# Layer 3's feed-forward part inside its edge sweep, and the first gathers of each sweep issued in the phase before

## The chip, the cores and the metric

One core of one Trainium2 chip. The time is the device time of one execution in microseconds, the median of three. The program is written engine by engine: TensorE (PE), VectorE (DVE), ScalarE (ACT), GpSimd (POOL) and SyncE (SP), each with its own instructions in a fixed order and semaphores between them.

## What is computed

A graph network on 6250 nodes of 128 features and 106250 directed edges, sorted by destination, self-loops included. Each layer takes h = relu(layernorm(x)) and adds its result to x.

```python
x = x + L0(h, edge_attr_64)            # relu(h[src] + e @ We + be) summed by dst, MLP, batch norm
x = x + L1(h)                          # mean of neighbours, one linear layer
# third layer (L2 in the names): GATv2, 8 heads
m      = leaky_relu(xl[src] + xr[dst] + edge_attr_128 @ W_e, 0.2)
logits = einsum('eho,ho->eh', m, att)
exl    = exp(logits - segment_max(logits, dst)[dst])
out    = segment_sum(xl[src] * exl / (segment_sum(exl, dst)[dst] + 1e-16), dst) + b_att
h2     = layer_norm(h + out, g1, be1)
result = layer_norm(h2 + gelu(h2 @ W1 + b1) @ W2 + b2, g2, be2)
# fourth layer: two GAT convolutions (4 heads, then 1) with elu behind each
```

## The kernel before

The edges are cut into 208 groups of 512 (four tiles of 128). Five sweeps walk over them, and between or inside them the work by nodes is done: `term_sweep` (first layer), `norm1_phase`, `sum_sweep` (second), `soft_sweep` for number 2 (the third layer, GATv2), `ffn_phase` (its feed-forward part), and `soft_sweep` for numbers 3 and 4 (`narrow_layers`, from L529). "Layer 3's sweep" is below the sweep of number 2.

Every sweep is a software pipeline in steps. At step t each engine does its part for group t, and later parts for groups t-1 to t-8 (LAG = 7). `sweep16` (L138) writes the first steps out, then a loop of 16 steps a round, then the rest. The order inside a step is the order of the code in the function `step` of that engine, written by hand. Four groups make a batch (BATCH), for which logits, running maxima and exponentials are taken together, one lane a head and group, 32 lanes for 8 heads.

POOL only gathers: for each tile an indirect DMA brings 128 source rows (L1792), into a ring of 16 groups. It waits until the group 16 back has been used (`message`).

In layer 3's sweep, TensorE's step (L1937 to L1977) is:

- `edge_terms(t)`: four transposes of gathered rows (L1867), then the matmul of edge attributes (L1873, 128x512) and that of destination rows (L1874).
- `scatter(t-7)`: four matmuls of one-hot by message into 64 partitions of a bank (L1908).
- `head_logits(t-1)`: one matmul, 32 columns by 512 (L1881).
- `flip_window(t-7)`: after ScalarE has copied the window (L1834), two transposes (L1930, L1931). VectorE adds the result to `sums` (`add`, L2016).
- once a batch: a shift (L1940), a carry (L1956), the weights turned edge-major (L1963) and factors (L1969, L1970).

VectorE's step is: leaky ReLU of t-1 (L2075), `add(t-8)`, `weigh(t-7)` (L2066), running maxima of the batch, the z-add of t (L2094), and the carry. ScalarE's: copies of weights, z (L1829), window (L1834) and lanes, and the exponentials.

In the sweeps of numbers 3 and 4 work by nodes is already part of the sweep: chunks of 256 nodes, 25 in all (`CN`, `NCH`), one stage of a chunk at a step (`node_steps`, L158). Chunk c may start at step 8(c + 4), since by then no later edge reaches its nodes (`BEHIND` = 4). Such a sweep ends 31 steps after the last group. Layer 3's does not: it ends after LAG more steps, and `ffn_phase` (L2421) works on 13 chunks of 512 nodes.

Each phase ends with `phase_end` (L68): its semaphores are cleared and all engines meet at a barrier. SP waits before it until the tables for the next sweep are stored. Only then does the next phase's first gather start.

## Time and profile before

| | |
|---|---|
| median of 3 runs | 7460.23 us (7456.46 to 7462.33) |
| span of the profiled execution, first to last instruction | 5796.6 us |
| difference, outside the span | 1663.6 us |
| mean granted TensorE clock | 0.779 |
| busy in the span: PE, DVE, ACT, POOL | 79%, 47%, 21%, 69% |
| gathers of layer 3's sweep, first to last | 2282.0 to 3349.9 us |
| then without a gather until | 3621.1 us |

No other time is given for the profiled execution itself; its span is part of an execution like the three timed ones, and sums below are made against that span. The chain of work that ended last is followed only through the last sweeps, so it says nothing about layer 3; the stretches and timelines do.

### The profile page before, as it was taken

To read this page: it belongs to the slowest core of one execution; us is meant where nothing else is said; L and a number is where in the kernel's file an instruction comes from. 1 tells how busy PE (TensorE), PEld (TensorE's weight loads), DVE (VectorE), ACT (ScalarE), POOL (GpSimd) and SP (SyncE) were. 2 spreads that over 40 slices of the span, in tenths; PEclk is the share of its full clock that TensorE was granted. 3 is DMA by queue.
4 is the path that set the end of the run, shared out by engine and by line. 5 is a ranking of instruction groups with operands and counts; after the bars stand their busy time and mean duration, and the time that the engine had idled before them with its cause. 6 is when DMAs were issued, how large, how long until landed. Compare 5 with 4: busy or idle time off the path is not lost. (4 is left out here: it accounts for less than half of the span.)

```text
span 5796.6 us, 89863 instructions
## 1 busy us (share of the span) xinstructions
PE 4596.1 (79%) x21959; PEld 3153.3 (54%) x21959; DVE 2702.8 (47%) x8105; ACT 1216.6 (21%) x3182; POOL 3988.9 (69%) x4207
## 2 busy tenths in 40 slices
PE   5888888657777776999999977687777758887887
PEld 4777777535556564444444433455555535555555
DVE  4222222321111113677777766555555545555555
ACT  2111111221211211222222258111111111111111
POOL 6777777457777775777777700777777747777775
PEclk9999999975555555999999989666666666666665
DMA  5333333244444443555555510455555534444443
GB/s 151 106 105 105 105 104 104 74 150 106 112 114 107 118 114 90 160 165 165 165 165 164 166 38 24 109 114 114 113 114 115 113 77 107 111 109 110 109 111 78
DMA packets 559823, 663.58 MB, mean 114 GB/s; under 512 B 196431, under 2 KB 390909, under 8 KB 558717
## 3 DMA queue, kind: packets, MB, share of 16 engines
q1 hardware_dynamic: 424909, 382.99, 22.2%
q0 software_dynamic: 134640, 277.80, 21.1%
q14 instruction: 207, 1.70, 0.1%
q8 instruction: 67, 1.10, 0.1%
HBM read 580.95 MB, written 86.19 MB: 115 GB/s over the span
## 5 line engine op out<-in xcount | busy, mean ns | idle before, releaser
L1792 POOL DMA_INDIRECT soft_rows<-table,sources x2496 | 2388.6, 957 | 1128.2 <-issue 737.7
L1422 POOL DMA_INDIRECT sum_rows<-table,sources x832 | 785.7, 944 | 343.9 <-issue 249.6
L1088 POOL DMA_INDIRECT term_rows<-table,sources x832 | 791.4, 951 | 289.4 <-issue 289.4
L1923 PE MATMUL psum<-soft_onehot,soft_message 128*128 128x64 f32 x3328 | 647.6, 358 | 107.1 <-DVE soft_message L2066 105.0
L1923 PEld LDWEIGHTS psum<-soft_onehot,soft_message 128*128 128x128 f32 x3328 | 586.1, 266 | 188.0 <-issue 181.8
L1119 PE MATMUL psum<-term_onehot,term_term 128*128 128x64 f32 x1664 | 403.9, 425 | 188.5 <-DVE sums L1171 176.6
L1464 PE MATMUL psum<-sum_onehot,sum_rows 128*128 128x64 f32 x1664 | 360.4, 391 | 222.7 <-DMA sum_rows<-table,sources 218.4
L1119 PEld LDWEIGHTS psum<-term_onehot,term_term 128*128 128x128 f32 x1664 | 370.7, 328 | 242.1 <-issue 242.0
L1165 DVE TENSOR_TENSOR term_term<-psum,term_rows 128x512 f32<-128x512 f32 x208 | 143.9, 692 | 753.0 <-issue 349.0
L1464 PEld LDWEIGHTS psum<-sum_onehot,sum_rows 128*128 128x128 f32 x1664 | 343.5, 304 | 278.0 <-issue 273.8
L1919 PEld LDWEIGHTS psum<-soft_onehot,soft_weights 128*4 128x4 f32 (+1 forms) x3328 | 284.9, 109 | 305.9 <-issue 293.0
L1109 PE MATMUL psum<-L_We,term_attrs 64*128 64x128 f32 x1664 | 430.5, 438 | 8.4 <-DMA term_attrs<-in_ea64T 8.4
L2066 DVE TENSOR_TENSOR soft_message<-soft_rows,psum 128x512 f32<-128x512 f32 x624 | 418.0, 670 | 2.9 <-issue 2.9
L1892 PE MATMUL psum<-soft_onehotT,soft_dst_cols 128*16 128x512 f32 (+1 forms) x416 | 375.4, 1004 | 49.4 <-DMA soft_dst_cols<-adst 49.4
L1109 PEld LDWEIGHTS psum<-L_We,term_attrs 64*128 64x128 f32 x1664 | 370.0, 325 | 56.4 <-issue 28.6
L1919 PE MATMUL psum<-soft_onehot,soft_weights 128*4 128x64 f32 (+1 forms) x3328 | 358.5, 272 | 12.4 <-DVE weight_sums L2011 0.9
L1097 ACT ACTIVATE term_term<-term_term 128x512 f32<-128x512 f32 x208 | 130.9, 630 | 913.0 <-DVE term_term L1165 913.0
L2016 DVE TENSOR_TENSOR sums<-sums,psum 128x64 f32 x624 | 136.7, 219 | 380.3 <-PE psum L1923 320.5
L1898 PE MATMUL psum<-ident,soft_src_cols 128*16 128x128 f32 (+1 forms) x832 | 173.5, 379 | 175.9 <-ACT soft_src_cols L1806 174.5
L1441 ACT ACTIVATE sum_flat<-psum 64x512 f32<-64x512 f32 x208 | 122.7, 590 | 830.9 <-PE psum L1454 826.4
L1503 DVE TENSOR_TENSOR sums<-sums,psum 128x64 f32 x208 | 46.2, 222 | 530.0 <-PE psum L1465 526.8
L1908 PEld LDWEIGHTS psum<-soft_message,soft_onehot 128*64 128x64 f32 x1664 | 188.1, 139 | 139.6 <-issue 138.8
(277 smaller groups left out, 6619.9 us busy)
## 6 DMA issues: line engine op xcount, KB each, us to landing
soft_onehotT<-onehotsT SPq DMA_DIRECT2D x312, 256.0 KB
soft_onehot<-onehots SPq DMA_DIRECT2D x624, 128.0 KB, 2.1
soft_attrs<-in_ea128T SPq DMA_DIRECT2D x208, 256.0 KB
soft_rows<-table,sources POOLq DMA_INDIRECT x2496
term_attrs<-in_ea64T SPq DMA_DIRECT2D x208, 128.0 KB, 2.8
onehots<-term_onehot SPq DMA_DIRECT2D x208, 128.0 KB
sum_onehot<-onehots SPq DMA_DIRECT2D x208, 128.0 KB, 2.7
onehotsT<-sum_flat SPq DMA_DIRECT2D x208, 128.0 KB
```

Source lines behind the costliest of these rows:

```text
L1088: pool.indirect_dma_start(rows[:, k, t, :], None, io.table0[0:NCH * CN], bass.IndirectOffsetOnAxis(sb.sources[:, g * TPG + t:g * TPG + t + ...
L1109: last = pe.matmul(term_bank[g.slot(4)][:, piece(b)], attrs[:, g.slot(AHEAD), piece(b)], sb.L0_We, start=True, stop=True)
L1119: last = pe.matmul(window[q], term[:, g.slot(4), b, :], onehot[:, g.slot(8), b], start=b == 0, stop=b == TPG - 1)
L1422: pool.indirect_dma_start(rows[:, k, t, :], None, io.table1[0:NCH * CN], bass.IndirectOffsetOnAxis(sb.sources[:, g * TPG + t:g * TPG + t + ...
L1464: pe.matmul(window[q], rows[:, g.slot(AROUND), b, 0:D], onehot[:, k, b], start=b == 0, stop=b == TPG - 1)
L1792: pool.indirect_dma_start(rows[:, k, t, :], None, table[0:NCH * CN], bass.IndirectOffsetOnAxis(sb.sources[:, g * TPG + t:g * TPG + t + 1], ...
L1892: pe.matmul(lane_bank[g.half()], dst_cols[:, j // 2], onehotT[:, pair(g)], start=j == 1, stop=False).then_inc(s.edge_term, 2)
L1898: last = pe.matmul(lane_bank[g.half()][:, piece(b)], src_cols[:, b], sb.ident, start=False, stop=b == TPG - 1)
L1908: last = pe.matmul(window_bank, onehot[:, k, b], message[:, g.slot(2), b, :], start=b == 0, stop=b == TPG - 1)
L1919: pe.matmul(bank[0:H, P:P + W], weights[:, q, b, j::BATCH], onehot[:, k, b], start=b == 0, stop=b == TPG - 1)
L1923: last = pe.matmul(bank[:, 0:W], message[:, g.slot(4), b, :], onehot[:, k, b], start=b == 0, stop=b == TPG - 1)
L2066: v.tensor_tensor(message[:, g.slot(2 if full else 4), :, 0:D].rearrange("p t (h c) -> p t h c", h=H), rows[:, g.slot(AROUND), :, 0:D].rea ...
```

## The change

`soft_sweep` for number 2 becomes a function of its own, `gatv2_sweep`, with `FfnNodes` in place of `ffn_phase`. In it:

- the feed-forward part of a chunk of 256 nodes is 22 stages at steps 8(c + 4) + 2 to + 24; the sweep ends 41 steps after the last group. One PSUM bank (4) is free for it, so
- the logits of a batch are four matmuls taken together, the one of group j writing partitions 32j to 32j + 31 of one bank, and lanes, starts, continuations and maxima use 128 partitions (8 of each 32);
- the scatter's four matmuls go in turn to partitions 0 to 63 and 64 to 127 of the window bank, and the flip is a matmul with `fold` (two identities stacked), which adds the halves;
- weights are turned by matmuls with `quad_pick`, not by transposes; starts and continuations are loaded by four DMAs each instead of one;
- several tiles share space with weights of layers that are done; the one-hot ring has two pairs instead of four.

In all sweeps the ring of gathered rows is one tile for all phases (`Ahead`). Group 0 of the sweeps of numbers 1 to 4 is gathered by POOL at the end of the phase before, once the table is stored, and each such sweep starts with group 1. The wait for the second table (`beside`) stays on SP. The very last tile gathers 16 rows, not 128.

```diff
+class Ahead:
+    def gather(self, pool, g):
+        k = g % AROUND
+        for t in range(TPG):
+            real = slice(0, P if (g * TPG + t) * P < E else 16)
+            pool.indirect_dma_start(self.rows[real, k, t, :], None, self.table,
...
-    soft_sweep(nc, io, sb, 2)
-    ffn_phase(nc, io, sb)
-    soft_sweep(nc, io, sb, 3)
-    soft_sweep(nc, io, sb, 4)
...
+        gatv2_sweep(nc, io, sb, to2, to3)
+        to4 = Ahead(nc, sb, ring, "soft4", io.table4, D + 1)
+        soft_sweep(nc, io, sb, 3, to3, to4)
+        soft_sweep(nc, io, sb, 4, to4, None)
...
             @block.gpsimd
             def _(pool):
-                for g in range(G):
+                for g in range(1, G):
...
+                nodes.table_stored(pool)
+                ahead.gather(pool, 0)
...
+class FfnNodes:
+    def act_steps(self, act, t):
+        node_steps(act, t, (2, self.stage), (4, self.norm1.take_root), (6, self.normalise1), (7, self.scaled1), (8, self.gelus(0)), (9, self.gelus(1)),
+                   (12, self.copy_res), (13, self.norm2.take_root), (14, self.normalise2), (19, self.norm3.take_root), (20, self.normalise3),
+                   (21, self.copy_h), (22, self.rows_out))
+    def pe_steps(self, pe, t):
+        node_steps(pe, t, (3, self.to_nodes), (7, self.flip_hh), (8, self.ups(0)), (9, self.ups(1)), (10, self.down), (12, self.flip_res),
+                   (21, self.flip_h), (22, self.project))
+    def dve_steps(self, v, t):
+        node_steps(v, t, (3, self.attention), (5, self.norm1.scale_shift), (10, self.residual), (12, self.statistics2), (13, self.norm2.scale_shift),
+                   (15, self.to_x), (19, self.norm3.scale_shift))
...
+def gatv2_sweep(nc, io, sb, of, ahead):
...
+    LAST = STEPS * (NCH - 1 + BEHIND) + 24
...
+                def head_logits(g):
+                    pe.wait_ge(s.leaky, g.times(1, BATCH))
...
+                    for j in range(BATCH):
+                        last = pe.matmul(lane_bank[j * QUAD:(j + 1) * QUAD], sb.att_cols, z[:, j], start=True, stop=True)
...
+                    for b in range(TPG):
+                        last = pe.matmul(window_bank[b % 2 * W:b % 2 * W + W], onehot[:, k, b], message[:, g.slot(2), b, :], start=b < 2, stop=b >= TPG - 2)
...
+                def flip_window(g):
+                    pe.wait_ge(s.window_copied, g.times(1, 1))
...
+                    pe.matmul(window_T[:, 0:W], window[:, 0:D], fold, start=True, stop=True)
+                    pe.matmul(window_T[0:H, P:P + W], window[:, D:D + H], fold, start=True, stop=True).then_inc(s.window_T, 1)
+
+                def step(t):
+                    if t.back(BATCH).closes(0):
+                        head_logits(t.back(BATCH))
+                    if t.exists():
+                        edge_terms(t)
+                    nodes.pe_steps(pe, t)
+                    g = t.back(BATCH + 2)
+                    if g.closes(0):
...
+                        pe.matmul(init_bank, shift.rearrange("h j a -> h (j a)"), sb.ones[0:H, 0:1], start=True, stop=True).then_inc(s.init_psum, 1)
+                    g = t.back(LAG)
+                    if g.exists():
+                        scatter(g)
+                        flip_window(g)
```

In ScalarE's new step the chunk's stages stand ahead of the window copy; in VectorE's they stand behind the z-add of t, ahead of the next step's leaky ReLU.

How this moves TensorE's instructions in layer 3's sweep: one plain step in the loop of the kernel before (L1867 starts `edge_terms`, L1881 is the logits).

```order
L1867 MATMUL psum<-ident,soft_rows 128x128 x4
L1873 MATMUL psum<-soft_attrs,L_We 128x512
L1874 MATMUL psum<-soft_onehotT,soft_dst_rows 128x512
L1904 REGISTER_ALU
L1905 REGISTER_ALU
L1908 MATMUL psum<-soft_message,soft_onehot 64x136 x4
L1881 MATMUL psum<-soft_z,att 32x512
L1930 MATMUL psum<-ident,soft_window 128x64
L1931 MATMUL psum<-ident,soft_window 8x64
```

The same place in the changed kernel, a step that carries a batch's logits and the transposes of a chunk's residual (`ring` is the ring of rows, L1864 `flip_res`, L2166 the scatter, L2173 and L2174 the flips).

```order
L2156 MATMUL psum<-soft_z,att_cols 32x512 x4
L2141 MATMUL psum<-ident,ring 128x128 x4
L2147 MATMUL psum<-soft_attrs,L_We 128x512
L2148 MATMUL psum<-soft_onehotT,rel_group 128x512
L1861 REGISTER_ALU
L1864 MATMUL psum<-ident,L_W 128x128 x2
L2166 MATMUL psum<-soft_message,soft_onehot 64x136 x4
L225 REGISTER_ALU
L2173 MATMUL psum<-L_W,soft_window 128x64
L2174 MATMUL psum<-L_W,soft_window 8x64
```

The logits, one matmul between scatter and flips in each step, are four at the head of every fourth step; nothing stands between scatter and flips now.

VectorE in the changed kernel, from the message of one group over the z-add and the stage `to_x` (L1884 to L1716) to the end of the loop's round; the leaky ReLU of the same group (L2312) is the first instruction behind the branch.

```order
L2298 TENSOR_TENSOR soft_message<-ring,psum 128x4x128
L2304 REGISTER_ALU
L2306 TENSOR_TENSOR soft_z<-psum,soft_z 128x512
L1884 TENSOR_TENSOR hT<-hT,L_g 128x256
L1886 TENSOR_TENSOR hT<-hT,L_be 128x256
L1888 ISA
L1888 TENSOR_TENSOR x_nodes<-x_nodes,hT 128x256
L1709 BN_STATS soft_ln_stat<-x_nodes 128x6
L1709 ISA
L1709 BN_STATS soft_ln_stat<-x_nodes 128x6
L1713 BN_AGGR soft_ln_mean_var<-soft_ln_stat 128x2 x2
L1716 TENSOR_SCALAR soft_ln_mean_var<-soft_ln_mean_var 128x2
```

Before, the z-add (L2094) was followed by the leaky ReLU (L2075) with nothing between in three steps of four; now a stage of up to nine instructions can stand there.

## Rows read from the trace of the kernel before

**Rows 1.** Timeline, POOL's gathers: start, length, line; in brackets the idle time before.
```profile
2499.68 0.94 POOL L1792 DMA_INDIRECT soft_rows<-table,sources  x1 [0.30 <-issue]
2500.93 0.94 POOL L1792 DMA_INDIRECT soft_rows<-table,sources  x1 [0.31 <-issue]
...
3621.07 0.94 POOL L1792 DMA_INDIRECT soft_rows<-table,sources  x1 [271.15 <-POOLq L71]
...
4710.41 0.94 POOL L1792 DMA_INDIRECT soft_rows<-table,sources  x1 [49.78 <-POOLq L71]
```

**Rows 2.** Busy time by stretch: length, PE, PEld, DVE, ACT, POOL, granted clock, DMA share, GB/s.
```profile
1195.70:2234.70 1039.00, 761.98 (x3438) 591.66 (x3438) 182.95 (x768) 199.06 (x617) 785.70 (x832) 0.57 0.45 118
2282.00:3349.90 1067.90, 1032.21 (x4586) 478.99 (x4586) 763.12 (x1934) 306.48 (x846) 814.50 (x832) 0.99 0.56 165
3406.00:3621.10 215.10, 151.43 (x572) 81.09 (x572) 145.66 (x561) 176.50 (x352) 0.04 (x1) 0.91 0.07 17
3621.10:4660.60 1039.50, 798.06 (x4655) 564.20 (x4656) 581.61 (x1752) 149.15 (x438) 786.23 (x832) 0.67 0.50 113
```

**Rows 3.** Timeline, TensorE, one plain step of layer 3's sweep: start, length.
```profile
3350.09 0.66 PE L1867 MATMUL psum<-ident,soft_rows 128*128 128x128 f32 x4
3350.59 1.02 PE L1873 MATMUL psum<-soft_attrs,L_We 128*128 128x512 f32 x2
3351.54 1.12 PE L1874 MATMUL psum<-soft_onehotT,soft_dst_rows 64*128 64x512 f32 x2
3352.59 1.14 PE L1908 MATMUL psum<-soft_message,soft_onehot 128*64 128x136 f32 x8
3353.66 1.05 PE L1881 MATMUL psum<-soft_z,att 128*32 128x512 f32 x2
3354.64 0.27 PE L1930 MATMUL psum<-ident,soft_window 64*128 64x64 f32 x1
...
3354.90 0.66 PE L1867 MATMUL psum<-ident,soft_rows 128*128 128x128 f32 x4
```

**Rows 4.** Timeline, TensorE: the sweep's first transposes, and the once-a-batch work.
```profile
2290.05 1.09 PE L1867 MATMUL psum<-ident,soft_rows 128*128 128x128 f32 x4 [14.31 <-DMA soft_rows<-table,sources]
...
3367.13 0.22 PE L1940 MATMUL psum<-ones,soft_shift 8*32 8x1 f32 x2
...
3369.83 0.40 PE L1963 MATMUL psum<-ident,soft_lanes 32*128 32x32 f32 x4 [0.17 <-ACT soft_lanes L1838]
...
3370.65 0.66 PE L1867 MATMUL psum<-ident,soft_rows 128*128 128x128 f32 x4
```

**Rows 5.** Timeline, TensorE, tail of layer 3's sweep, after its last edge terms.
```profile
3381.69 0.24 PE L1930 MATMUL psum<-ident,soft_window 64*128 64x64 f32 x1 [0.46 <-ACT soft_window L1834]
...
3398.92 2.05 PE L1908 MATMUL psum<-soft_message,soft_onehot 128*64 128x136 f32 x8 [1.12 <-DVE soft_message L2066]
...
3402.99 2.04 PE L1908 MATMUL psum<-soft_message,soft_onehot 128*64 128x136 f32 x8 [1.12 <-DVE soft_message L2066]
```

**Rows 6.** Groups by line, VectorE, layer 3's sweep: count, busy us, mean ns, idle before.
```profile
L2075 DVE SCALAR_TENSOR_TENSOR soft_z<-soft_z 128x512 f32<-128x512 f32 x203 | 139.6, 688 | 31.7 <-issue 26.9
L2094 DVE TENSOR_TENSOR soft_z<-psum,soft_z 128x512 f32<-128x512 f32 x203 | 137.7, 678 | 111.5 <-PE psum L1874 111.4
```

**Rows 7.** Prices of node work: timelines of the feed-forward phase, and one group by line.
```profile
3441.04 3.70 PE L2544 MATMUL psum<-ffn_gelu,L_W 128*128 128x512 f32 x8 [1.21 <-ACT ffn_gelu L2477]
...
3447.28 1.64 ACT L287 ACTIVATE ffn_h<-x_nodes,ffn_ln_shift,ffn_ln_rstd 128x128 f32<-128x128 f32 x4
...
3447.71 0.87 DVE L262 BATCH_NORM_STATS2 ffn_ln_stats<-ffn_res 128x6 f32<-128x128 f32 x4
...
3458.35 1.09 PE L2563 MATMUL psum<-L_W1x,ffn_h_out 128*128 128x136 f32 x8
...
L1566 DVE TENSOR_TENSOR soft_val<-soft_val,L_b 128x256 f32<-128x256 f32 x50 | 21.3, 427 | 1.7
```

**Rows 8.** Timeline, SP: the feed-forward phase's last table store.
```profile
3615.21 0.37 SPq L2635 DMA_DIRECT2D table<-ffn_rows  x1
```

More of the change, by code:

```diff
@@ L42 @@
 BATCH = 4
+QUAD = P // BATCH
 LAG = BATCH + 3
@@ L1648, in dve_steps, with past @@
         node_steps(v, t, (2, self.ratio), (4, self.combine))
-def soft_sweep(nc, io, sb, layer):
-    H = {2: 8, 3: 4, 4: 1}[layer]
-    L, W = H * BATCH, NARROW
-    full = layer == 2
-    table, width = {2: (io.table2, D), 3: (io.table3, D + 4), 4: (io.table4, D + 1)}[layer]
-    dst_table, dst_width = {2: (io.xr_table, D), 3: (io.adst3, 4), 4: (io.adst4, 2)}[layer]
-    spread = {2: sb.lane_expand8, 3: sb.lane_expand4, 4: sb.ones}[layer]
-    mask, heads = sb.lane_mask[0:L], sb.lane_head[0:L, 0:H]
-    AHEAD = 4
-    DST = AHEAD if full else BATCH
-    phase = f"soft{layer}"
-    FIRST = AROUND if full else 4 * AROUND
-    LAST = G + LAG if full else STEPS * (NCH - 1 + BEHIND) + 14
-    names = ("order cleared starts_in cont_in rows_T rows_out edge_term z leaky src_out logits lanes_out running backward fend carry_psum carry shift init_psum init maxima "
+def past(eng, sem, c, n=1):
+    if c.i is not None or c.base >= 1:
+        eng.wait_ge(sem, c.times(n))
@@ L1672, in tile @@
             return ctx.enter_context(nc.sbuf_tensor(f"{phase}_{name}", shape, dt))[:]
-        rows = tile("rows", [P, AROUND, TPG, width])
+        rows, gathered = of.rows, of.gathered
+        onehot = tile("onehot", [P, 4, TPG, W])
+        onehotT = tile("onehotT", [2 * W, 2, GE])
+        message = tile("message", [P, 2, TPG, D + H])
+        starts = tile("starts", [P, GE + 1])
+        cont = tile("cont", [P, GE])
+        lanes = tile("lanes", [P, GE])
+        weights = [half.rearrange("p (t l) -> p t l", t=TPG) for half in (sb.L0_be, sb.L0_W1)]
@@ new lines, in gatv2_sweep, with added, side, pair @@
+        factor_head_bank = sb.psum[0:H, 7, 48:48 + BATCH]
+        nodes = FfnNodes(nc, io, sb, tile, sb.psum[:, 4, :])
+        CLEARED = 6
+        ORDER = 4
+        def added(act, t):
+            g = t.back(LAG + 2)
+            if t.i is None and g.base >= G:
+                g = At(None, G - 1, AROUND)
+            act.wait_ge(s.order, g.times(ORDER, ORDER))
+        def side(g):
+            return slice(g.slot(2) * W, g.slot(2) * W + W)
+        def pair(g):
+            return g.slot(4) // 2
@@ new lines, in gatv2_sweep, with soft_sweep, tile @@
+    phase_end(nc, tuple(s) + nodes.all_sems + (gathered,))
+def soft_sweep(nc, io, sb, layer, of, ahead):
+    H = {3: 4, 4: 1}[layer]
+    L, W = H * BATCH, NARROW
+    table, width = {3: (io.table3, D + 4), 4: (io.table4, D + 1)}[layer]
+    dst_table, dst_width = {3: (io.adst3, 4), 4: (io.adst4, 2)}[layer]
+    spread = {3: sb.lane_expand4, 4: sb.ones}[layer]
+    mask, heads = sb.lane_mask[0:L], sb.lane_head[0:L, 0:H]
+    AHEAD = 4
+    phase = f"soft{layer}"
+    FIRST = 4 * AROUND
+    LAST = STEPS * (NCH - 1 + BEHIND) + 14
+    names = ("order cleared starts_in cont_in edge_term leaky src_out logits lanes_out running backward fend carry_psum carry shift init_psum init maxima "
+             "shifted factor_log weights_lane factor spread weights_T weights_out factor_psum factor_out message "
+             "scattered").split()
+    s = sems(nc, phase, *names, dst_rows=BATCH, onehotT=4, onehot=4)
+    with ExitStack() as ctx:
+        def tile(name, shape, dt=F32):
+            return ctx.enter_context(nc.sbuf_tensor(f"{phase}_{name}", shape, dt))[:]
+        rows, gathered = of.rows, of.gathered
@@ L1711, in soft_sweep @@
         factor_head_bank = sb.psum[0:H, 7, 48:48 + BATCH]
-        nodes = None if full else GatNodes(nc, io, sb, tile, layer, sb.psum[:, 2, :])
-        CLEARED = 4 + (not full)
+        nodes = GatNodes(nc, io, sb, tile, layer, sb.psum[:, 2, :])
+        CLEARED = 5
         ORDER = 4
@@ L1809, in step @@
                 def step(t):
-                    if not full and t.back(BATCH).closes(0):
+                    if t.back(BATCH).closes(0):
                         take_sources(t.back(BATCH))
@@ L1846, in step @@
                     if g.closes(0):
-                        act.wait_ge(s.logits, g.times(1, BATCH) if full else g.uses(BATCH))
+                        act.wait_ge(s.logits, g.uses(BATCH))
                         if g.back(BATCH).exists():
@@ L1899, in src_logits @@
                     last.then_inc(s.logits, 1)
-                def scatter(g):
-                    k = g.slot(4)
-                    wait_past(pe, s.window_copied, g, 1, 0)
-                    pe.wait_ge(s.onehot[k], g.uses(4, 16))
-                    pe.wait_ge(s.columns, g.times(1, 1))
-                    pe.wait_ge(s.message, g.times(1, 1))
-                    for b in range(TPG):
-                        last = pe.matmul(window_bank, onehot[:, k, b], message[:, g.slot(2), b, :], start=b == 0, stop=b == TPG - 1)
-                    last.then_inc(s.scattered, 1)
                 def scatter_T(g):
@@ L2071, in step @@
                 def step(t):
-                    g = t.back(1)
-                    if g.exists() and full:
-                        v.wait_ge(s.z, g.times(1, 1))
-                        v.scalar_tensor_tensor(z[:, g.slot(2)], z[:, g.slot(2)], 0.2, z[:, g.slot(2)], ALU.mult, ALU.max).then_inc(s.leaky, 1)
                     g = t.back(LAG)
```

792 lines of the change are left out of this document (627 added, 165 removed).

## The prediction

> **What bounds the kernel now.** I read the granted clock and the busy time by stretch first, then the timeline of the gather queue, then TensorE's timeline in layer 3's sweep, then the lines of the feed-forward phase. All my sums are in the time of the profiled execution: its span is 5796.6 us. The runs' median is 7460.23 us, so 1663.6 us lie outside the span, which nothing in the profile itemises; I take that part as unchanged and add differences of the span to the median. This measurement tells about 0.2% (15 us) from no change.
>
> Four of the five sweeps run at the pace of the gathers. One gather starts 1.25 us after the last [rows 1], four make a group of 512 edges, so a step costs 5.0 us and 208 steps 1039 us, as the stretches of layers 2 and 4 show [rows 2]. Layer 3's sweep is the exception: 1067.9 us from first to last gather, with TensorE busy 1032 us at a clock of 0.99. TensorE's starts in one plain step are 4.81 us apart (3350.09 to 3354.90): 0.50 transposes, 0.95 and 1.05 the two term matmuls (together with the transposes 2.50, "edge terms" below), 1.07 the scatter, 0.98 the attention logits, 0.26 the two window flips [rows 3]. A batch of four steps takes 3350.09 to 3370.65, which is 20.56 us or 5.14 per step; 1.32 of it is work done once per batch [rows 3, 4]. So there TensorE, not the gather queue, sets the pace, with hardly any slack: 20.56 against 20.0 per batch. Then come 271.2 us without a gather [rows 1], of which the feed-forward phase with its hand-over is 3406 to 3621, 215 us for 25 chunks of 256 nodes, or 8.6 us per chunk, with TensorE busy for 151 [rows 2].
>
> **The change, part by part.**
> It removes the 215 us phase. In return, every eight steps of layer 3's sweep carry one chunk's 22 stages, for the 174 steps from step 34 on. Let P be the time of eight such steps. Before, eight steps took 41.1.
>
> TensorE's work in eight new steps:
> - edge terms 8 x 2.50 = 20.0, unchanged [rows 3].
> - scatter: the four matmuls now go in pairs to two halves of the output partitions. Bounds: 1.07 as now, and half of it, 0.55. I take 0.60, as each matmul keeps its shape of 64 columns: 4.8.
> - logits: four matmuls together per batch, each into its own 32 partitions. Bounds: one at 0.98, and four in a row at 3.9 [rows 3]. I take 1.1, near the lower end, since each uses a quarter of the array's columns, which the row of 0.98 leaves idle: 2.2. No row shows two such matmuls side by side, so both bounds stay in the range.
> - window flips are no longer transposes; four passes, by the pace of 128x136 matmuls (eight in 1.09, so 0.12 each) for the wide pair [rows 7] and half of that for the narrow: 0.40 instead of 0.26, so 3.2.
> - turning the weights edge-major was four transposes in 0.40 [rows 4]; now four full matmuls of two passes each, eight times 0.12: 1.0. With the factors 0.35, carry and shift 0.3: 3.3 for two batches.
> - a chunk's node work: up and down, 16 passes of 256 columns at half of the 0.45 that 512 take (3.70 for eight) [rows 7] = 3.7; eight transposes at 0.13 = 1.0, denominators 0.2, projection 0.5, and about 0.1 at each of eight starts: 6.3.
> Together 39.8 us, as much as the gathers' 40.0. So any wait on TensorE lengthens the sweep.
>
> The Trainium skill, "TensorEngine Tiling (Array Packing)", Theoretical Speedup and Key Properties, says that column tiles run in parallel, up to 4 times faster for 32 columns and 2 times for 64, and that a switch of the tiling mode drains the array. By its full factor the logits would cost 0.98 and the scatter 0.53, which would move P by less than 1 us; the drain speaks against the change and is not separately visible in any row here.
>
> Now the waits, eight steps numbered 0 to 7 by what they carry, walked on TensorE, VectorE and ScalarE with the durations of the rows (0.1 from TensorE's end to a reader, 0.15 from a reader's end back to TensorE):
> - The logits stood between scatter and flips and covered ScalarE's copy of the window. Without them TensorE waits 0.46 after the scatter's end, as the tail of today's sweep shows where it has no logits to do [rows 5]; from the last issue that is 0.53. 8 x 0.53 = 4.3.
> - The batch's logits stand first in steps 0 and 4 and need the leaky ReLU of the group just before. On VectorE that stands behind the z-add (0.68) and the nodes' stage of step 7 or 3. Those are three 256-wide operations at 0.43, two statistics at 0.22, aggregates and small ones, 2.35 in all [rows 7], or the attention stage and a scale-shift, 2.65. From the end of the edge terms the logits can start after 0.11 + 0.68 + 2.35 + 0.8 + 0.15 = 4.1 us, while TensorE has only 1.9 us of other work. Wait 2.15 each time [rows 6]: 4.3.
> - In steps 2 and 6 the weights need shift, subtract, exponential: 2.7 us from the shift matmul to the transposes now [rows 4], of which TensorE fills 1.7; with the exp table load behind the window copy in step 6, 1.5 each: 3.0.
> - ScalarE's node stages stand ahead of the window copy: two gelus in each of steps 0 and 1 and copy and normalise (four blocks took 1.64, two take 0.83 [rows 7]) in step 4 delay the flips by 0.25, 0.25 and 0.75: 1.3. In step 6 VectorE comes late with the message by 1.15.
> P = 39.8 + 4.3 + 4.3 + 3.0 + 1.3 + 1.15 = 53.9 us against 41.1. **A chunk thus costs 12.8 us inside the sweep, where it cost 8.6 outside.** The 34 steps without nodes come to 5.2 each by the same walk: what packing gives, the uncovered waits take.
>
> The tail: the sweep runs on to step 248, 41 steps past the last group. Eight still scatter (4.07 each, 3398.92 to 3402.99 [rows 5]) = 33. For the 33 with node work alone I take the pace of the present tails: from the last gather of layer 4's first sweep 49.8 us to the next, of which 5.9 are hand-over, for 31 steps, 1.43 each [rows 1, 8] = 47. Bounds for the whole 41: 59 and 100. Hand-over 5.9.
>
> The sum. Before, from the first transpose of layer 3 at 2290.05 [rows 4] to the next layer's first gather at 3621.07 [rows 1]: 1331 us. After: 34 x 5.2 + 174 x 53.9 / 8 + 80 + 6 = 177 + 1172 + 86 = 1435: **+104 us.**
>
> The early gathers: at four boundaries POOL issues group 0's four gathers, 5.0 us of its queue, once the table has landed, and joins the barrier behind them. From the last table store's issue to the next gather 5.86 us pass now [rows 1, 8]; landing comes first, so at most some 3.5 us of barrier can lie beside the 5.0 of issuing. But the barrier also waits for POOL, so the second group is gained little: I take 2 per boundary, bounds 0 and 3.5. 4 x 2 = **-8 us**. A gather's pace decides in three of those sweeps; in the fourth TensorE does.
>
> Costed at nothing, with their cover: the 16-row gather at the very end, the eight small DMAs per batch for starts and continuations instead of two (on SP, whose issues of 0.4 us leave it over half idle) and three more memsets at the start cost nothing while SP runs three steps ahead; without that cover about 2.5 us per batch. SP's node store waits for the rows in step 0 and is queued ahead of the loads, which still are a step early.
>
> 7460 + 104 - 8 = 7556; I give **7555**. The 96 is also the bound of comparison below.
>
> **The rivals.**
> Faster: the walk's waits do not come. If VectorE's node stages end before the logits are due (P falls by 4.3) and flips and weights find their inputs sooner (by 4), P is about 45.5: 104 - 21.75 x 8.4 = -79, with the early gathers -87: **7373**. It decides at P = 49.5, where gain and loss are equal (96 / 21.75 = 4.4 below the walk). For it: TensorE's bare work is only 39.8, the gathers need 40.0, and today's sweep waits almost nowhere. With P at 40 it would be 7254. Against it: the 0.46 wait is in the trace, and the order is fixed on every engine. Chance 0.29.
> Slower by more: the packed matmuls run one after the other. Logits +2.8 twice, scatter +0.47 eight times, P = 63.3, +204: **7760**. For it: no row shows packing. Chance 0.18.
> The clock: the sweep of layer 2, with TensorE busy 73%, was granted 0.57 and that of layer 4 0.67; the feed-forward phase, at 70%, 0.91 [rows 2]. With 74% busy the new sweep could fall from 0.99 to 0.9 now and then, adding about 3 to P, 65 us: **7620**. Both levels, 2.4 and 1.2 GHz, would be seen. Chance 0.15 (slower too).
> No change: P near 49.5. Chance 0.05.
> The forecast itself: 0.33, own range 7490 to 7600.
>
> **How the numbers follow.** Slower by over 0.2% are the forecast, packing's failure and the clock: 0.33 + 0.18 + 0.15 = 0.66. Faster 0.29, same 0.05. Range: down into the faster rival to P = 45, 7370, up to packing's failure with a longer tail, 7780; outside are a full overlap and both evils at once, 2 in 10.
>
> **What would show it.** Right: no stretch without gathers between layers 3 and 4 beyond about 100 us; layer 3's gathers waiting on the message; TensorE's starts about 6.7 us per step with waits named after the leaky ReLU and the window copy; feed-forward lines inside the sweep. The logits' four matmuls starting within 1.2 us show packing, 3.9 its absence. Wrong: steps under 6.1 us, or gathers 1.25 us apart all through layer 3.

## The result, and the profile after

The changed kernel takes 7558.41 us (median of four, 7545.65 to 7573.27), the kernel before 7458.34; the ratio is 1.0134 with a 95% interval of 1.0114 to 1.0154. So it is slower by 100 us where +96 was forecast. The agreement is worth little: large errors of both signs cancelled, as the runs below show.

The mean clock and span of the profiled execution of the changed kernel:

```profile
core 0: 7546.3 us, clock 0.706
```

This span and its device time (7549.88) differ by 3.6 us. Nothing like 1663.6 us lies outside it. That number, on which the prediction built its bridge from span to median, was no part of an execution: the profile shown of before came from another one.

The gathers of the changed kernel at the ends and starts of sweeps (POOL's timeline), to be held against [rows 1]:

```profile
2708.83 0.86 POOL L307 DMA_INDIRECT ring<-table,sources  x1 [0.31 <-issue]
2802.75 0.95 POOL L307 DMA_INDIRECT ring<-table,sources  x1 [93.06 <-DMA table<-sum_node_rows]
2818.52 0.94 POOL L307 DMA_INDIRECT ring<-table,sources  x1 [11.06 <-POOLq L71]
...
4478.11 0.86 POOL L307 DMA_INDIRECT ring<-table,sources  x1 [0.30 <-issue]
4640.75 0.95 POOL L307 DMA_INDIRECT ring<-table,sources  x1 [161.79 <-DMA table<-rel_group]
4656.52 0.94 POOL L307 DMA_INDIRECT ring<-table,sources  x1 [11.07 <-POOLq L71]
```

Layer 3's gathers last from 2802.75 to 4478.11, 8.2 us per step in the middle of the sweep, then come 161.8 us without one. Stretches of the same trace (columns as in [rows 2]): the middle of the sweeps of layer 2 and layer 3, the tail of layer 3's, the middle of layer 4's first.

```profile
1500.00:2650.00 1150.00, 648.33 (x3002) 515.83 (x3003) 148.33 (x671) 170.25 (x538) 703.56 (x746) 0.54 0.33 88
2920.00:4450.00 1530.00, 1243.77 (x5476) 637.18 (x5475) 819.77 (x2394) 511.34 (x1270) 724.58 (x754) 0.76 0.38 107
4480.00:4640.00 160.00, 109.95 (x484) 63.80 (x482) 77.46 (x275) 68.32 (x167) 0.00 (x0) 0.72 0.13 35
4700.00:5980.00 1280.00, 812.33 (x4333) 580.07 (x4334) 529.21 (x1621) 134.12 (x404) 730.01 (x774) 0.61 0.36 85
```

Even the sweep of layer 2, which the change hardly touches, makes 746 gathers in 1150 us, 1.54 us each, not 1.25. Either the change had slowed all five sweeps, or these executions ran under another condition than the profile of before. That was the first question.

### The profile page after: what moved, and what is told of

It is laid out like the page before. It is cut to its first block and busy times, and to the rows that moved or that the text cites. A ratio compares the mean times of both kernels' runs of the same rounds, so it can differ in the third digit from the quotient of the medians.

```text
span 7546.3 us, 92357 instructions
## 1 busy us (share of the span) xinstructions
PE 4861.8 (64%) x22761; PEld 3376.0 (45%) x22761; DVE 2697.3 (36%) x8270; ACT 1314.4 (17%) x3425; POOL 3976.7 (53%) x4212
## 5 line engine op out<-in xcount | busy, mean ns | idle before, releaser
L307 POOL DMA_INDIRECT ring<-table,sources x4160 | 3950.8, 950 | 3486.7 <-issue 1162.2
L2540 PE MATMUL psum<-soft_onehot,soft_message 128*128 128x64 f32 x3328 | 700.9, 380 | 465.3 <-DVE soft_message L2667 422.2
L2540 PEld LDWEIGHTS psum<-soft_onehot,soft_message 128*128 128x128 f32 x3328 | 637.0, 286 | 553.1 <-issue 545.9
L1189 DVE TENSOR_TENSOR term_term<-psum,ring 128x512 f32<-128x512 f32 x208 | 143.4, 689 | 1009.7 <-remote 734.1
L1493 PE MATMUL psum<-sum_onehot,ring 128*128 128x64 f32 x1664 | 348.4, 383 | 232.1 <-issue 94.5
L1493 PEld LDWEIGHTS psum<-sum_onehot,ring 128*128 128x128 f32 x1664 | 343.2, 303 | 259.1 <-issue 253.1
L2147 PE MATMUL psum<-soft_attrs,L_We 128*128 128x512 f32 x416 | 307.3, 832 | 13.9 <-issue 5.9
L2501 ACT ACTIVATE soft_lanes<-psum 16x512 f32<-16x512 f32 (+1 forms) x104 | 61.0, 587 | 1373.5 <-PE psum L2525 921.8
L2148 PE MATMUL psum<-soft_onehotT,rel_group 64*128 64x512 f32 x416 | 298.1, 804 | 0.0
L2306 DVE TENSOR_TENSOR soft_z<-psum,soft_z 128x512 f32<-128x512 f32 x208 | 143.2, 688 | 412.9 <-PE psum L2148 287.7
```

What stands on the lines that cost most here:

```text
L307: pool.indirect_dma_start(self.rows[real, k, t, :], None, self.table, bass.IndirectOffsetOnAxis(self.sb.sources[real, g * TPG + t:g * TPG ...
L1189: v.tensor_tensor(term[:, g.slot(4)], term_bank[g.slot(4)].rearrange("p (t n) -> p t n", t=TPG), rows[:, g.slot(AROUND)], ALU.add).then_in ...
L1493: pe.matmul(window[q], rows[:, g.slot(AROUND), b, 0:D], onehot[:, k, b], start=b == 0, stop=b == TPG - 1)
L2147: pe.matmul(term_bank, sb.L2_We, attrs[:, k], start=True, stop=False)
L2148: pe.matmul(term_bank, dst_rows[side(g), k], onehotT[side(g), pair(g)], start=False, stop=True).then_inc(s.edge_term, 1)
L2306: v.tensor_tensor(z[:, g.slot(BATCH)], term_bank, z[:, g.slot(BATCH)], ALU.add).then_inc(s.z, 1)
```

## The experiments

### Which condition is timed?

The kernel before, unchanged:

> The kernel before, unchanged, profiled once more. Theory A (the prediction's: 1664 us lie outside the span, the span itself is typical): span about 5800 us, every sweep of layers 1, 2 and 4 at 5.0 us per step, device time about 7460. Theory B (the profile shown of before came from a faster execution than the timed ones, and little lies outside a span): span within 10 us of the device time, about 7455, with the sweeps of layers 1, 2 and 4 at 6.0 to 6.7 us per step as in the changed kernel's profile, and layer 3's sweep of before well above 5.14 us per step.

Measured: 5799.7 us, span 5797.4, beside 5801.0 for a second execution of the same kernel. Neither theory: the whole device time was 5800, 2.3 us outside the span. The changed kernel, unchanged, next:

> The changed kernel, unchanged, on the chip on which the kernel before took 5800 us. Theory A (the change costs what the prediction's sum says, +96, and the rest of the 1660 us by which the timed runs of before exceeded its profile belongs to a condition of the chip that slows both kernels alike): 5895 us, layer 3's sweep at 6.7 us per step, the sweeps of layers 1, 2 and 4 at 5.0. Theory B (the sum is right by accident; in the undisturbed condition the new sweep walks at 5.5 to 6.0 us per step): 5690 to 5790 us.

Measured: 7551.5 (7546.3 to 7569.5) with 7465.1 for before. The chips, or their surroundings, have two conditions, so both kernels had to be traced on one chip:

> The kernel before once more, for its trace on the chip of the runs beside it. Two kinds of chip have been met: on one (7460 us) the changed kernel's gathers pause about 4 us after every 12 or 16 of them, on the other (5800 us) the gathers of the kernel before run 1.25 us apart without a pause. Theory A (the pauses are the chip's, whatever the kernel): where the device time is about 7460, this trace shows the same pauses in all five sweeps, 1.0 to 1.7 us more per step in the sweeps of layers 1, 2 and 4, and layer 3's sweep at 7.5 to 8.0 us per step. Theory B (the pauses come with the shared ring of the changed kernel): no such pauses, 5.0 us per step in four sweeps, whatever the device time.

Measured: 7468.8, span 7466.6. Theory A, except that layer 3's sweep is quicker than the 7.5 to 8.0 it named: the old kernel is slowed as well. Steps in the middle of its five sweeps take 6.0, 6.15, 7.19, 6.66 and 6.64 us (POOL's gathers of groups 34 to 175, 141 steps), against 5.03, 5.0, 5.14, 5.0 and 5.01 in the profile shown ahead. What is late shows at the start of the first sweep: VectorE's add of the gathered rows, groups 4 to 6 (timeline of the kernel before in this run):

```profile
103.78 0.69 DVE L1165 TENSOR_TENSOR term_term<-psum,term_rows 128x512 f32<-128x512 f32 x1 [20.44 <-remote]
...
148.81 0.69 DVE L1165 TENSOR_TENSOR term_term<-psum,term_rows 128x512 f32<-128x512 f32 x1 [43.87 <-remote]
...
184.03 0.69 DVE L1165 TENSOR_TENSOR term_term<-psum,term_rows 128x512 f32<-128x512 f32 x1 [34.07 <-remote]
```

The run at 5800 us has them at 86.49, 91.36 and 96.39. PE's edge terms of these groups were long done, so what is awaited is the gathered rows. POOL issues on at 1.25 us until the ring is full: 23 groups are out when group 8 is added, at 189.1; in the profile shown ahead nine and a half, at 107.1. What DMA moved in 40 equal slices from 600 to 900 us (GB/s), first in the changed kernel's late profile, then in the profile of before shown ahead:

```profile
GB/s 105 83 55 128 41 114 87 86 102 87 74 113 36 131 70 79 108 87 61 126 89 37 140 87 35 134 85 62 121 72 86 106 35 149 87 44 114 78 53 140
```

```profile
GB/s 122 87 108 101 121 89 102 108 101 109 110 101 99 111 87 122 96 110 100 105 105 105 87 122 87 106 108 118 87 122 87 124 87 107 102 109 101 110 100 106
```

In the first, the gather queue's packets stop 14 times for 3.8 to 4.8 us, each time after 12 or 16 gathers. I call this the **late** condition, the other the **prompt** one. Why the landings are late is not settled; it is not tied to one chip (one was met in both conditions) nor to the kernel. All timed runs of the result are late ones; the profile the prediction read is prompt.

> The changed kernel on the same chip. On a chip of 5800 us for the kernel before: by the prediction's walk layer 3's sweep at 6.7 us per step and 5895 us in all; if TensorE's waits are hidden as the faster rival had it, 5.7 per step and 5710. On a chip of 7460: 7550, layer 3's sweep at 8.3 us per step.

Measured, late: 7555.5 (7551.0 to 7573.4), 8.13 us per step. Once more, alone:

> The changed kernel alone, one look. It is to meet the condition in which the kernel before takes 5800 us and its gathers run 1.25 us apart without pauses. If the condition comes: the prediction's walk gives 5895 us with layer 3's sweep at 6.7 us per step; the faster rival 5710 with 5.7 us per step; and, since the trace of the changed kernel shows its early gathers holding the barrier up, about 25 us more than the walk's sum (5920). If it does not come: 7550 with 8.1 us per step.

Measured, late again: 7567.4.

### What do the node stages cost, and what the rearranged edge part?

```diff
-    LAST = STEPS * (NCH - 1 + BEHIND) + 24
+    LAST = G + LAG + 1
-                    node_steps(sp, t, (24, nodes.store))
-                    nodes.act_steps(act, t)
-                    nodes.pe_steps(pe, t)
-                    nodes.dve_steps(v, t)
```

> All 22 node stages of layer 3 are left out of its sweep, which ends with group 208 (the feed-forward part, the residual and layer 4's table are not computed; three copies of another table stand in for it, so what layer 4 works on is different data of the same size). It shows what the rearranged edge part alone costs per step. On a chip of 5800: the walk's 5.2 us per step against 5.14 before; if packing gains more than the uncovered waits take, 5.0, the gathers' pace. On a chip of 7460: theory A (node stages are what lengthens layer 3's sweep) 6.3 to 6.8 us per step, as in layers 2 and 4; theory B (the edge part itself is the bound, with the clock at half) 7.5 or more.

Measured, one execution, late, on the chip of the two traces above (7330.6 us in all): 7.25 us per step by POOL's gathers, where before has 7.19 and the changed kernel 8.13. POOL runs ahead of the others by up to a ring of 16 groups, so TensorE's own starts are the better measure: from step 34 to step 207 they give 7.25, against 7.07 before and 8.23 in the changed kernel. So in this condition packing, the longer flips and the uncovered waits together cost 0.18 per step, and the node stages 0.98, or 7.8 us per chunk. Theory A has the cause right; the step itself is longer than the 6.3 to 6.8 it named.

The clock fell before any node work was there: from 3200 to 3800 us it was 0.86 in the kernel before, 0.76 in this one and 0.77 in the changed kernel.

### The logits' place

```diff
-                    if t.back(BATCH).closes(0):
-                        head_logits(t.back(BATCH))
                     if t.exists():
                         edge_terms(t)
+                    if t.back(BATCH).closes(0):
+                        head_logits(t.back(BATCH))
```

> The batch's four logit matmuls stand behind the edge terms of their step instead of ahead of them. Theory A (the wait on the leaky ReLU at the head of every fourth step is on the path, 2.15 us each, 52 times): 50 to 110 us faster than the changed kernel. Theory B (another engine or the gathers decide there, and TensorE only waits because it is early): within 20 us of the changed kernel. Theory C (ScalarE's copy of z must now wait for the logits, and delays the z-add): 20 to 100 us slower.

Measured, late: 7602.4 (7591.9 to 7606.3), 47 us slower than the changed kernel beside it, 8.51 us per step. Theory C. TensorE's wait for the leaky ReLU is all but gone, 2.3 us from 3200 to 3800 us where the changed kernel has 34.1, and the time is longer all the same. Other waits of that stretch (engine, line, releaser: us in total, times, longest):

```profile
ACT soft_z L2105 <- PE psum L2156: 76.0, 14, 7.7
PE psum L2173 <- ACT soft_window L2113: 70.4, 49, 6.6
```

The first is new: ScalarE's copy of z, 14 times 5.4 us behind the logits; with it the window copy is later and TensorE's flips wait 70.4 us instead of 32.2.

### The early gathers

```diff
-                for g in range(1, G):
+                for g in range(0, G):
...
-                nodes.table_stored(pool)
-                ahead.gather(pool, 0)
```

> The changed kernel without its early gathers: each sweep's POOL gathers its own group 0 first, behind the barrier, as before. Layer 3's sweep and its node stages stay. Theory A (the prediction's step: early gathers save 2 us at each of four boundaries): 8 us slower than the changed kernel, 7563 where the kernel before takes 7465. Theory B (read from the trace of the changed kernel: the barrier of the phase does not open until some 10 us after POOL's four early gathers, so that group 1 and all other engines start about 7 to 9 us later than before at three of the boundaries): 20 to 27 us faster than the changed kernel, 7530 where before takes 7465, with the gap from a sweep's last gather to group 1's first back at about 92 us (before) from 102 (changed) between the last two sweeps. On a chip where before takes 5800: 5870 by the walk of the prediction, under 5800 if TensorE's waits are hidden there.

Measured, late: 7547.5 (7514.7 to 7566.7), before 7461.3: ratio 1.0125 (1.0105 to 1.0146). All thirteen times of the changed kernel lie between 7545.7 and 7573.4, so the total doesn't decide. The boundary does. First the changed kernel (the profile after), the last stores of layer 4's first sweep, POOL's first early gather, and its first of group 1:

```profile
6093.91 0.47 SPq L1661 DMA_DIRECT2D adst<-soft_node_rows  x1
...
6095.90 0.95 POOL L307 DMA_INDIRECT ring<-table,sources  x1 [84.80 <-DMA table<-soft_node_rows]
...
6111.78 0.94 POOL L307 DMA_INDIRECT ring<-table,sources  x1 [11.20 <-POOLq L71]
```

and the kernel before, late:

```profile
6021.83 0.47 SPq L1630 DMA_DIRECT2D adst<-soft_node_rows  x1
...
6028.24 0.95 POOL L1792 DMA_INDIRECT soft_rows<-table,sources  x1 [86.61 <-POOLq L71]
```

From the store to group 1's first gather 17.9 us pass now; before 6.4 to group 0 and, four gathers on, 11.4. The early gathers start 4 us sooner, but POOL leaves the barrier only 11.2 us after the last of them, and all engines with it. Without early gathers the gap from last gather to group 1 is 95.5 us here (99.4 to 102.1 in four traces of the changed kernel, before 92.6), and ahead of layer 3 it is 102.0 (changed 109.6 to 111.7, before 101.6). Theory B, at the boundaries. Only at the first boundary is there no such hold-up (changed kernel, prompt):

```profile
1199.01 0.94 POOL L307 DMA_INDIRECT ring<-table,sources  x1 [3.55 <-POOLq L71]
```

No run shows what the barrier waits for, nor why the first one differs.

### Where TensorE waits

Three edits, in one run on one chip, and then the changed kernel on another. All met the prompt condition, before at 5800.5 and 5801.0.

```diff
                     if t.exists():
                         edge_sum(t)
+                    g = t
+                    if g.exists():
+                        v.wait_ge(s.z, g.times(1, 1))
+                        v.scalar_tensor_tensor(z[:, g.slot(BATCH)], ...).then_inc(s.leaky, 1)
                     nodes.dve_steps(v, t)
```

> In VectorE's step the leaky ReLU of group t follows its z-add directly, ahead of the node stage, instead of coming first in the next step. Theory A (the walk's term: TensorE waits on the leaky ReLU at the head of every fourth step because a node stage stands ahead of it; the trace of the changed kernel shows 34.1 us in 18 such waits, 1.89 each): nearly all of 2 x 1.89 = 3.8 us per eight steps goes, 22 times over: 80 us faster than the changed kernel, 7475 where it takes 7555. Theory B (the time is only shifted: the node stages and what waits for them come later by the same amount, or the wait turns up at another line of TensorE): within 20 us of the changed kernel.

```diff
-                    nodes.pe_steps(pe, t)
...
                         scatter(g)
+                    nodes.pe_steps(pe, t)
                         flip_window(g)
```

> TensorE's node stage of a step stands between scatter and flips, where the logits stood before, and ScalarE copies the window ahead of its node stages. Theory A (the walk's terms 4.3 and 1.3: since nothing stands between scatter and flips TensorE waits there for the window copy; the trace shows 51.7 us in 73 such waits, 0.71 each): 5 us per eight steps go, 22 times: 110 us faster than the changed kernel, 7445 where it takes 7555. Theory B (the node stages' own chain over the engines, or the gathers that land late, set the pace and TensorE's waits only move): within 20 us. Theory C (node results come too late for VectorE and ScalarE of the same step): 20 to 60 us slower.

> Both of the former edits together, and no early gathers. Theory A (the three costs are separate and add up): 80 + 110 + 20 = 210 us faster than the changed kernel, 7345, which is 110 us faster than the kernel before. Theory B (TensorE's waits are not what lengthens the sweep): within 40 us of the changed kernel and slower than the kernel before. Layer 3's sweep: 7.1 us per step by A, 8.0 by B.

> The changed kernel once more. If it meets the condition in which the kernel before takes 5800 us, it is the missing base of the three edits before it (6067 with the leaky ReLU next to the z-add, 6166 with the node stages between scatter and flips, 6013 with both and without early gathers). Theory A (the wait for the leaky ReLU is on the path; covering the window copy by node stages is not worth anything, because it delays what reads them): 6130 to 6170, layer 3's sweep at 7.5 us per step, clock in it well below 1.0. Theory B (the walk's sum): 5895 with 6.7 per step, and then both edits made it slower. If it meets the other condition: 7553, layer 3's sweep at 8.1 us per step, and the size of the edits stays open.

Measured: changed kernel **6163.9** (6151.0 to 6173.7), ratio to before 1.0618 (1.0602 to 1.0635); leaky ReLU moved 6067.1; node stages under the window copy 6165.6; both and no early gathers 6013.0, still 1.0363 (1.0346 to 1.0381) of before. So in the condition of the profile the change costs 363 us, not 96, and no version here beats the kernel before.

Busy time of the changed kernel, prompt: the stretch in which POOL gathers groups 8 to 48 and TensorE walks steps 7 to 38, with hardly any node stage yet; then 152 steps with them (gathers of groups 48 to 200, TensorE's steps 40 to 191).

```profile
2330.00:2530.00 200.00, 175.83 (x842) 89.78 (x840) 124.60 (x327) 53.30 (x146) 152.26 (x156) 0.81 0.52 150
2535.00:3743.00 1208.00, 979.38 (x4515) 502.69 (x4515) 681.09 (x2023) 447.06 (x1097) 579.51 (x608) 0.81 0.41 110
```

The second is 19 times eight steps: 63.6 us each. Clock 0.81, where the kernel before has 0.99 [rows 2]. TensorE's groups of that stretch that wait (count, busy, mean ns, idle before and its releaser):

```profile
L2166 PE MATMUL psum<-soft_message,soft_onehot 128*64 128x136 f32 x1216 | 116.8, 318 | 0.6 <-DVE soft_message L2298 0.6
L2173 PE MATMUL psum<-L_W,soft_window 128*128 128x64 f32 x304 | 68.3, 310 | 103.0 <-ACT soft_window L2113 103.0
L2156 PE MATMUL psum<-soft_z,att_cols 128*32 128x512 f32 x304 | 65.8, 949 | 77.6 <-DVE soft_z L2312 77.6
L2204 PE MATMUL psum<-quad_pick,soft_lanes 128*128 128x32 f32 x304 | 44.9, 294 | 47.4 <-ACT soft_lanes L2123 47.4
```

228.6 us of waits: 12.0 per eight steps. With the leaky ReLU moved, the same 152 steps take 1107 us:

```profile
L2166 PE MATMUL psum<-soft_message,soft_onehot 128*64 128x136 f32 x1216 | 116.3, 317 | 31.1 <-DVE soft_message L2298 30.9
L2173 PE MATMUL psum<-L_W,soft_window 128*128 128x64 f32 x304 | 67.5, 307 | 88.5 <-ACT soft_window L2113 85.9 <-DVE sums L2245 1.9 <-DVE weight_sums L2247 0.7
L2156 PE MATMUL psum<-soft_z,att_cols 128*32 128x512 f32 x304 | 57.2, 795 | 0.3
L2204 PE MATMUL psum<-quad_pick,soft_lanes 128*128 128x32 f32 x304 | 48.0, 307 | 47.3 <-ACT soft_lanes L2123 47.3
```

The waits fall to 167.2, by 61 us. The stretch falls by 101, since the clock also rises (0.81 to 0.84) and TensorE's busy time sinks from 979 to 940. The whole is 97 us faster: Theory A. With the node stages under the window copy (1197 us, clock 0.76):

```profile
L2166 PE MATMUL psum<-soft_message,soft_onehot 128*64 128x136 f32 x1216 | 119.2, 323 | 32.9 <-DVE soft_message L2299 32.5
L2156 PE MATMUL psum<-soft_z,att_cols 128*32 128x512 f32 x304 | 72.5, 1042 | 105.2 <-DVE soft_z L2313 105.2
L2173 PE MATMUL psum<-L_W,soft_window 128*128 128x64 f32 x304 | 65.4, 301 | 8.1 <-ACT soft_window L2110 7.7
...
L2205 PE MATMUL psum<-quad_pick,soft_lanes 128*128 128x32 f32 x304 | 55.8, 338 | 76.1 <-ACT soft_lanes L2123 76.1
```

Of the 103 us at the flips 95 are gone, and 89 have come back elsewhere: leaky ReLU +28, weights +29, message +32. Theory B. That wait was no cost of its own; that it was slack of a loop over three engines is how I read it. Both together: 167 us of waits, as with the leaky ReLU alone, 1088 us for the 152 steps. In all that run is 151 us faster than the changed kernel, between its theory A (210) and B (within 40): the leaky ReLU alone gave 97, the boundaries ahead of layer 3 and of the last sweep give 12 (52.8 and 58.3 us from last gather to group 1, changed 60.5 and 62.5), and the rest is not assigned to one edit.

## Why the prediction came out

**The time outside the span: wrong.** The step "1663.6 us lie outside the span, I take that part as unchanged" failed. Every execution whose span is on record beside its time has 1.6 to 5.7 us outside, in both conditions. Here is the whole difference, each from the gathers' timelines, in us:

| stretch | late, 7466.6 to 7548.1 | prompt, 5796.6 to 6162.0 |
|---|---|---|
| up to the last gather of layer 2 | -5.0 | -1.7 |
| to group 1 of layer 3 | +10.0 | +7.2 |
| to layer 3's last gather | +176.3 | +451.0 |
| to layer 4's first gather | -118.0 | -108.1 |
| to its group 1 | +10.7 | +10.7 |
| to its last gather | -4.7 | -0.4 |
| to group 1 of its second sweep | +9.5 | +6.8 |
| rest | +2.6 | -0.1 |
| sum | +81.4 | +365.4 |

The mechanism is the same in both, and is the one forecast: the phase goes, layer 3's sweep pays more than it gave. In the late condition the sweep of before had itself been lengthened, from 5.22 to 7.07 us per step by TensorE's starts (steps 34 to 207), the changed one's only from 7.93 to 8.23. That, and not the sum of the prediction, is why +100 was measured. The forecast had +280 for the sweep, -176 for what lies behind it and -8 for the boundaries; the late column has +176, -118, +30 and -7 elsewhere. That these sum to nearly the same is luck.

**The pace of the other four sweeps: right only in the prompt condition** (5.0 to 5.03 us per step; late 6.0 to 6.66), equally for both kernels.

**P = 53.9 us: work and waits nearly right, the clock wrong.** By TensorE's groups, us per eight steps (prompt: the 152 steps above; late: 3200 to 3800 us of both, 83 and 73 steps; records overlap, so the measured columns exceed the step by 5 to 6):

| | forecast | prompt | late, before | late, changed |
|---|---|---|---|---|
| edge terms | 20.0 | 29.1 | 26.5 | 30.0 |
| scatter | 4.8 | 6.1 | 10.3 | 6.3 |
| logits | 2.2 | 3.5 | 9.3 | 3.4 |
| flips | 3.2 | 6.0 | 4.2 | 6.0 |
| batch extras | 3.3 | 4.8 | 2.7 | 5.4 |
| node work | 6.3 | 7.6 | 0 | 7.8 |
| waits | 14.1 | 12.0 | 10.6 | 12.2 |
| eight steps | 53.9 | 63.6 | 57.8 | 65.8 |

The rows behind scatter, logits and flips in the late condition, before and then changed:

```profile
L1908 PE MATMUL psum<-soft_message,soft_onehot 128*64 128x136 f32 x664 | 107.3, 311 | 13.9 <-DVE soft_message L2066 13.0 <-issue 0.8
...
L1881 PE MATMUL psum<-soft_z,att 128*32 128x512 f32 x166 | 96.7, 668 | 0.0
...
L1930 PE MATMUL psum<-ident,soft_window 64*128 64x64 f32 x83 | 23.8, 286 | 91.1 <-ACT soft_window L1834 77.2 <-issue 13.9
```

```profile
L2166 PE MATMUL psum<-soft_message,soft_onehot 128*64 128x136 f32 x584 | 57.8, 326 | 1.5 <-DVE soft_message L2298 0.8 <-issue 0.6
L2173 PE MATMUL psum<-L_W,soft_window 128*128 128x64 f32 x146 | 33.2, 313 | 51.7 <-ACT soft_window L2113 32.2 <-issue 19.5
L2156 PE MATMUL psum<-soft_z,att_cols 128*32 128x512 f32 x144 | 31.3, 956 | 34.1 <-DVE soft_z L2312 26.1 <-issue 8.1
```

Before, too, TensorE waits there for the window copy, 1.1 us per step, beside a clock of 0.86.

Waits, term by term, prompt: flips and ScalarE's stages ahead of them 5.4 (forecast 4.3 + 1.3), leaky ReLU 4.1 (4.3), weights 2.5 (3.0), the message 0.03 (1.15). TensorE's busy time is 979.4 / 19 = 51.5, at a clock of 0.81 some 42 us of full speed, against 39.8 forecast. That 42 is a rough estimate: with the node stages under the window copy the same work took 974.7 us at 0.76, which would make it 39. The clock's part shows directly in the edge terms. In these 152 steps they took 3.31 us from their start to the next instruction's, between 2.48 and 4.76, where the walk had 2.50 in each step; that alone is 6.5 of the 9.7 us by which P was short. A slow step of that stretch has this matmul at half clock:

```profile
2950.31 1.91 PE L2147 MATMUL psum<-soft_attrs,L_We 128*128 128x512 f32 x2
```

It takes 1.02 in the fast step shown below under packing. So the term that failed is the 39.8 us of TensorE's work, priced at full clock throughout. The rival called "the clock" had the right cause and 3 us per eight steps, and it took nearly 10. I had compared shares of busy time between sweeps and set 0.9 "now and then". The sweep of before had TensorE busy 97.5% (975.93 of 1000 us from 2320) and a clock of 1.00.

What lowers the clock is not shown. It is already down where no node work stands (next paragraph), so the node stages are not the whole cause. The waits that opened when the logits left are the likely one, but their total does not decide it: with the node stages under the window copy they summed to 222 us and the clock was 0.76, in the changed kernel to 229 and it was 0.81.

**34 steps without nodes at 5.2: wrong in the prompt condition.** By TensorE's starts they took 201.6 us (2292.04 to 2493.62), 25 more than the 177 of the walk; before, the same 34 took 177.9. Steps 8 to 34 come to 5.82 us each (before 5.18). That stretch, columns as in [rows 2]:

```profile
2342.40:2493.60 151.20, 133.99 (x670) 69.15 (x666) 95.54 (x246) 38.66 (x109) 115.27 (x118) 0.84 0.54 152
```

TensorE is busy 89% and waits 17.2 us in 26 steps, at a clock of 0.84. The gathers do not set this pace: POOL brings groups 8 to 48 in 207 us, 5.18 each, only by running ahead, while TensorE walks 32 steps. So the rearranged edge part costs 0.6 us per step here before any node work is added. In the late condition the same steps take 7.27 before, 7.19 in the changed kernel and 7.24 without node stages: no loss in these steps.

**Packing: it works.** At full clock (first batches of the sweep, prompt) eight passes of the logits take what two took [rows 3]:

```profile
2341.43 1.07 PE L2156 MATMUL psum<-soft_z,att_cols 128*32 128x512 f32 x8
```

A scatter beside edge terms at full clock (both of L2147's passes in 1.02, as in [rows 3]):

```profile
2956.40 1.02 PE L2147 MATMUL psum<-soft_attrs,L_We 128*128 128x512 f32 x2
...
2959.38 0.69 PE L2166 MATMUL psum<-soft_message,soft_onehot 128*64 128x136 f32 x8
```

So the rival "packed matmuls run one after the other" falls (the walk had 1.1 and 0.60, the rows say 1.07 and 0.69), and the full factor that the Trainium skill gives ("TensorEngine Tiling (Array Packing)", Theoretical Speedup) agrees for 32 columns. The scatter's eight passes take 0.69 where they took 1.14 [rows 3], a factor of 1.65; there the page has up to 2. The late columns show what it brought, 9.9 us, and what became of it: flips and batch extras, the weights turned by full matmuls above all, +4.5, lower clock on the edge terms +3.5, waits +1.6, and the node work itself 7.8.

**The tail: 80 us forecast, 96 measured.** The last edge terms start at 3865.05, their step ends at 3871.0, and the last table store is at 3967.1 (prompt). The eight steps that still scatter took 34 us, as forecast (33); the 33 with nodes alone took 62, 1.9 each. The pace I took for them, 1.43 us per step, was that of layer 4's tails; a longer chain over the engines is the likely reason, and the clock is low there:

```profile
3850.00:3880.00 30.00, 23.86 (x131) 13.26 (x131) 19.99 (x59) 14.09 (x37) 0.00 (x0) 0.89 0.13 32
3880.00:3910.00 30.00, 21.39 (x102) 14.70 (x103) 15.89 (x67) 12.63 (x32) 0.00 (x0) 0.58 0.05 14
3910.00:3940.00 30.00, 17.37 (x47) 10.50 (x45) 9.43 (x41) 12.90 (x32) 0.00 (x0) 0.61 0.02 5
```

**The early gathers: wrong sign.** Forecast -2 at each of four boundaries; +7 to +11 at three, nothing at the first. The step that failed: "at most some 3.5 us of barrier can lie beside the 5.0 of issuing". The barrier took 11 us after the last gather.

**The faster rival** (walk's waits don't come) is refuted by the waits above. In the prompt condition layer 3 by TensorE's starts, from its first transpose to the next gather, is 201.6 for 34 steps (walk 177), 1377.4 for 174 (1172; 63.3 per eight), 96 for the tail (80) and 2.4 to the early gather (6): 1677 where the walk had 1435 and the kernel before 1331. That is +346; with +2 ahead of it, +11 and +7 at the two boundaries behind and -0.6 elsewhere it is the 365 measured.

## What to carry to other kernels

Hold a profile's own device time beside the timed median before anything else; if they differ by more than a few us, the profile shows another condition, and each step price needs a second trace. Moving a phase under a sweep is free only while the sweep's bound has room: here TensorE was at 97%, and a chunk that cost 8.6 us outside made its eight steps 22 us longer in the prompt condition (7.93 against 5.22 us per step) and 9 in the late one, part of it through a lower clock. A stretch by the issuing engine's timeline is not the pace of the engine that works: look at the latter's own starts. And a wait on the busiest engine is a cost only if its removal does not reappear two lines on: test it before counting it.

## What the runs showed of the hardware

- The same program took 5800 or 7465 us. In the slower executions the gathers' packets stopped for about 4 us after every 12 or 16 gathers, with the ring full; the reason is open.
- At three of four boundaries POOL left the barrier 11.1 to 11.2 us after its last of four indirect gathers (0.94 us of issue each), in both conditions, at the first 3.6; with no gathers ahead of the barrier, 5.9 us passed from the issue of the last table store to the next gather.
- Four matmuls of 32 columns, each into its own 32 partitions, took 1.07 us, as one did (1.05); four of 64 columns in two halves took 0.69 for 1.14.
- Removing 61 us of TensorE's waits gave 101: TensorE was also busy 40 us less, at a clock of 0.84 for 0.81.
